# Two plain sums of a graph kernel: ten tiles each fetched row by row from the sync engine and ScalarE

## What is computed

```
agg = jax.ops.segment_sum(x[src], dst, num_segments=N)         # first layer
h = (1.0 + eps) * x + agg
...
h = x @ W                                                      # last layer
msg = h[src] * norm[:, None]
out = jax.ops.segment_sum(msg, dst, num_segments=N) + b
```

## Time and profile before

| | us |
|---|---|
| median of 3 runs | 9637.63 |
| profiled execution, its own time | 9643.64 |
| span of the profiled execution | 9641.6 |
| first sum with the plan, first gather to last | 18.6 to 1158.7 |
| last sum, first gather to last | 8450.3 to 9577 |
| GpSimd busy, whole span | 5742.4 |

### The profile page before, as it was taken

The page is one execution under the profiler, slowest core; times in us unless marked ns, Lnnn a source line. Parts: engine busy times, 40 slices in busy tenths (PEclk is TensorE's granted clock), DMA queues, the critical chain, the costliest instruction groups (busy, mean ns, idle before and its releaser), DMA issues. The chain is left out here.

```text
span 9641.6 us, 93453 instructions
## 1 busy us (share of the span) xinstructions
PE 5106.8 (53%) x23452; PEld 3485.5 (36%) x23571; DVE 5124.3 (53%) x19615; ACT 1985.2 (21%) x5001; POOL 5742.4 (60%) x5738
## 2 busy tenths in 40 slices
PE   2332332444414444497777777777767777623223
PEld 2222322433413333343233333333356667513213
DVE  3233443444524444676777777777766666724225
ACT  0000021222212222310222222222234444500001
POOL 6676526666456666122666666666556666466765
PEclk7555665555555555698888889989979998855556
DMA  2111122222122222287666667766656666221111
GB/s 64 46 47 46 38 45 59 72 70 68 48 63 70 69 68 67 66 334 259 199 203 207 199 205 208 208 203 204 183 163 175 176 176 176 73 54 45 47 46 46
DMA packets 434195, 1155.57 MB, mean 120 GB/s; under 512 B 106036, under 2 KB 147476, under 8 KB 420744
## 3 DMA queue, kind: packets, MB, share of 16 engines
q0 software_dynamic: 295984, 849.83, 32.1%
q1 hardware_dynamic: 122892, 275.01, 8.5%
q10 hardware_dynamic: 14796, 24.75, 0.8%
HBM read 1016.65 MB, written 132.52 MB: 119 GB/s over the span
## 5 line engine op out<-in xcount | busy, mean ns | idle before, releaser
L953 POOL DMA_INDIRECT gat_ring<-gat_table,psrc_idx x1664 | 1645.6, 989 | 1120.5 <-issue 476.0
L589 DVE TENSOR_TENSOR acc<-acc,bank 128x129 f32 (+1 forms) x1664 | 480.1, 289 | 1475.1 <-remote 1252.9
L1938 POOL DMA_INDIRECT pair<-right_table,idx_r_idx x782 | 799.5, 1022 | 582.3 <-issue 183.6
L1148 DVE TENSOR_TENSOR acc<-acc,bank 128x130 f32 x1664 | 482.5, 290 | 1214.0 <-remote 847.1
L2098 POOL DMA_INDIRECT msg<-left_table,pidx_idx x832 | 799.7, 961 | 502.5 <-issue 203.0
L1938 POOL DMA_INDIRECT acc<-left_table,idx_l_idx x782 | 802.6, 1026 | 428.8 <-issue 219.1
L521 POOL DMA_INDIRECT gcn_sum_ring<-gcn_table,src_idx x782 | 790.2, 1011 | 369.5 <-issue 229.8
L521 POOL DMA_INDIRECT gin_sum_ring<-in_x,src_idx x782 | 769.0, 983 | 373.5 <-issue 226.5
L1017 PE MATMUL bank<-gat_ring,gat_hot 128*128 128x130 f32 x3328 | 765.7, 406 | 385.4 <-DVE gat_hot L1137 254.1
L2000 ACT ACTIVATE positive<-acc 128x512 f32<-128x512 f32 x782 | 492.4, 630 | 2022.2 <-DVE acc L2028 1358.7
L1977 PE MATMUL bank<-pair,ident 128*128 128x512 f32 x1564 | 874.9, 643 | 1.9 <-issue 1.5
(11 more groups left out here) (554 smaller groups left out, 9355.0 us busy)
## 6 DMA issues: line engine op xcount, KB each, us to landing
gat_place<-local_rows SPq DMA_DIRECT2D x128, 416.0 KB
left_table<-rel_out SPq DMA_DIRECT2D x49, 1032.0 KB, 4.9
right_table<-rel_out SPq DMA_DIRECT2D x49, 1032.0 KB, 3.9
feat<-attr_rows SPq DMA_DIRECT2D x194, 256.0 KB
gat_ring<-gat_table,psrc_idx POOLq DMA_INDIRECT x1664
types<-type_rows SPq DMA_DIRECT2D x98, 256.0 KB
msg<-left_table,pidx_idx POOLq DMA_INDIRECT x832
gin_sum_ring<-in_x,src_idx POOLq DMA_INDIRECT x782
```

Source lines behind the costliest of these rows:

```text
L953: e.indirect_dma_start(ring[:, at:at + TROW], None, table[:, :], bass.IndirectOffsetOnAxis(ap=ed["psrc"][:, i:i + 1], axis=0)).then_inc(*g ...
L1938: e.indirect_dma_start(to[j % NG][:, n * LROW:(n + 1) * LROW], None, tab[:, :], bass.IndirectOffsetOnAxis(ap=idx[:, i:i + 1], axis=0)).the ...
```

## The change

In both sums the tiles 118, 190, ..., 766 are fetched by the sync engine and the tiles 82, 154, ..., 730 by ScalarE: ten tiles each, every 72nd. GpSimd leaves them out. A new class `Singles` first loads the ten tiles' source rows as a list into SBUF (one DMA, one tile per partition). For each of its tiles it waits for the slot as GpSimd does, then 16 times loads eight row numbers into registers of its engine and issues eight DMAs of one row of 512 bytes each, whose place in the table is the register's value. Each adds 16 to one of two semaphores in turn. PE waits for the 128 landings of a tile before the batch that begins with or holds it. `gathered` counts how many gathers of GpSimd a batch's semaphore gets now. In the first sum the sync engine does this after the plan's store and ScalarE at once; in the last sum the sync engine does it ahead of the stores of the output, and ScalarE between `first_scalar` and `Ending.scalar`. The lists lie in 1 KB per partition: their own in the first sum, a part of an index table that is no longer needed in the last. One scratch tile of the plan now shares its place with another.

```diff
--- before.py
+++ after.py
@@ -38,6 +38,7 @@
 CHUNKS = PAIRS // CT
 RING = 128
 PLAN_AT = 40
+SP_TILES, ACT_TILES = (118, TILES, 72), (82, TILES, 72)
 GR = 13
 HQ = 4
 PAIR = 2
@@ -197,8 +198,8 @@
         self.k, self.c, self.ed, self.recs, self.local_rows = k, c, ed, recs, local_rows
         self.rec = sb("rec_i", G * 3 * P, I32)
         self.tile_i, self.tile_f = sb("tile_i", IT, I32), sb("tile_f", IT)
-        self.limit_i, self.limit, self.below = (sb(n, NB * G, d) for n, d in (
-            ("limit_i", I32), ("limit", F32), ("below", F32)))
+        self.limit_i, self.limit = (sb(n, NB * G, d) for n, d in (("limit_i", I32), ("limit", F32)))
+        self.below = self.limit_i[:, :].bitcast(F32)
         self.cnt, self.begins, self.block_col = sb("cnt", NB), sb("begins", 1), sb("block_col", 2 * G)
         self.passed, self.blk, self.tau, self.local, self.psrc, self.pidx, self.ends = (
             acc[:, j * SLOTS:(j + 1) * SLOTS] for j in range(7))
@@ -493,6 +494,43 @@
 
 
 
+class Singles:
+
+
+    def __init__(self, k, name, tiles, recs, table, ring, idx):
+        self.k, self.tiles, self.table, self.ring = k, tiles, table, ring
+        self.lists = recs[tiles.start:tiles.stop:tiles.step, 0:P]
+        self.idx = idx
+        self.landed = k.slots(f"{name}_dma", 2)
+        (self.listed,) = k.begin("loaded")
+
+    def fetch(self, e, engine, product):
+        e.dma_start(self.idx[0:len(self.tiles), :], self.lists).then_inc(*self.listed.up(16))
+        e.wait_ge(*self.listed.at(2, 16))
+        for n, i in enumerate(self.tiles):
+            free = slot_free(i)
+            if free:
+                e.wait_ge(*product.at(free))
+            at = i % RING * TROW
+            for q in range(0, P, BATCH):
+                row = self.k.regs(engine, self.idx[n:n + 1, :], q, BATCH, N - 1)
+                for j in range(BATCH):
+                    e.dma_start(self.ring[q + j:q + j + 1, at:at + F], self.table[bass.ds(row[j], 1), :]
+                                ).then_inc(*self.landed[n % 2].up(16))
+
+    def wait_tile(self, e, i):
+        if i in self.tiles:
+            n = self.tiles.index(i)
+            e.wait_ge(*self.landed[n % 2].at((n // 2 + 1) * P, 16))
+
+
+def slot_free(i):
+
+    b = i // HQ
+    free = min((b + 1) * HQ, TILES) - 1 - RING + NB
+    return max(0, -(-free // HQ))
+
+
 def aggregate_rows(k, c, ed, name, table, acc, width, plan=None, end=None):
     with ExitStack() as own:
         NQ, Q, NH, NP2, NBATCH = 22, HQ, 3, 3, PAIRS // HQ
@@ -503,6 +541,11 @@
         premade = lambda b: ENDS <= b < ENDS + late
         hot_of = lambda b: hot[NH + b - ENDS if premade(b) else b % NH]
         got = k.slots("pool_dma", NQ)
+        lists = k.sb(f"{name}_lists", 2 * P, I32, ctx=own)[:, :] if plan else ed["idx_l"][:, 0:2 * P]
+        singles = {ENG.SP: Singles(k, "sp", range(*SP_TILES), ed["recs"], table, ring, lists[:, 0:P]),
+                   ENG.Activation: Singles(k, "act", range(*ACT_TILES), ed["recs"], table, ring, lists[:, P:2 * P])}
+        one_by_one = {i for s in singles.values() for i in s.tiles}
+        gathered = lambda b: sum(i not in one_by_one for a in range(b % NQ, b + 1, NQ) for i in range(a * Q, a * Q + size(a)))
         filled, hot_made, product, added, chained, end_made = k.begin(
             "filled", "hot_made", "product", "added", "dve", "meaned")
         size = lambda b: min(Q, TILES - b * Q)
@@ -514,25 +557,30 @@
             def _(e):
                 for i in range(TILES):
                     b = i // Q
-                    free = b * Q + size(b) - 1 - RING + NB
-                    if i % Q == 0 and free > 0:
-                        e.wait_ge(*product.at(-(-free // Q)))
+                    if i % Q == 0 and slot_free(i):
+                        e.wait_ge(*product.at(slot_free(i)))
                     at = i % RING * TROW
-                    e.indirect_dma_start(
-                        ring[:, at:at + F], None, table[:, :],
-                        bass.IndirectOffsetOnAxis(ap=ed["src"][:, i:i + 1], axis=0)).then_inc(*got[b % NQ].up(16))
+                    if i not in one_by_one:
+                        e.indirect_dma_start(
+                            ring[:, at:at + F], None, table[:, :],
+                            bass.IndirectOffsetOnAxis(ap=ed["src"][:, i:i + 1], axis=0)).then_inc(*got[b % NQ].up(16))
                     if plan and i == PLAN_AT - 1:
                         plan.gpsimd(e)
 
-            if plan or end:
-                @block.sync
-                def _(e):
-                    (plan or end).sync(e)
-
-            if end:
-                @block.scalar
-                def _(e):
+            @block.sync
+            def _(e):
+                if plan:
+                    plan.sync(e)
+                singles[ENG.SP].fetch(e, ENG.SP, product)
+                if end:
+                    end.sync(e)
+
+            @block.scalar
+            def _(e):
+                if end:
                     end.first_scalar(e, filled)
+                singles[ENG.Activation].fetch(e, ENG.Activation, product)
+                if end:
                     end.scalar(e, added)
 
             @block.tensor
@@ -542,7 +590,10 @@
                 e.wait_ge(*filled.at(2 if width > F else 1))
                 for b in range(NBATCH):
                     if b * Q < TILES:
-                        e.wait_ge(*got[b % NQ].at(b // NQ * Q + size(b), 16))
+                        e.wait_ge(*got[b % NQ].at(gathered(b), 16))
+                        for i in range(b * Q, b * Q + size(b)):
+                            for s in singles.values():
+                                s.wait_tile(e, i)
                     if b * Q % BATCH == 0:
                         at = k.regs(ENG.PE, ed["ring_row"], b * Q, BATCH, (RING - 1) * TROW)
                     e.wait_ge(*(end_made.at(b - ENDS + 1) if premade(b) else hot_made.at(b + 1 - (late if b > ENDS else 0))))
@@ -1302,12 +1353,12 @@
         turned, out_v, out_s, loaded, dve = k.begin("turned", "out_v", "out_s", "loaded", "dve")
         att_split, packed, widened, gated, exped, typed = k.begin(
             "att_split", "packed", "widened", "gated", "exped", "typed")
-        part_out = k.slots("part_out", 3)
+        part_out = k.slots("act_dma", 3)
         attr_got, cast, residual, weights, firsts, laters, linear = k.begin(
             "attr_got", "cast", "residual", "weights", "left_loaded", "right_loaded", "linear")
         folded, fold, product, biased, lin_product, lin_biased = k.begin(
             "folded", "fold", "product", "biased", "lin_product", "lin_biased")
-        stored = k.slots("row_out", 2)
+        stored = k.slots("sp_dma", 2)
         with k.nc.Block() as block:
             @block.sync
             def _(e):
@@ -2556,7 +2607,7 @@
     with ExitStack() as ctx:
         k = Kernel(nc, ctx)
         c = make_constants(k)
-        ed = {"degree": k.sb("degree", NB)}
+        ed = {"degree": k.sb("degree", NB), "recs": w["recs"]}
         x, acc = k.sb("x_rows", NP), k.sb("acc", NB * ROW)
         with ExitStack() as early:
             with ExitStack() as own:
```

## The result

The changed kernel takes 10237.1 us (median of 4 runs, 10220.4 to 10257.7), the kernel before 9634.4 beside it: ratio 1.0633, interval [1.0611, 1.0654]. The forecast was 9584, the range ended at 9740.

The account below looks back on a forecast made before the run. GpSimd's issuing of gathers was taken to bound both sums, not the bytes. Profiled 9643.6 us minus 54 for 40 gathers, with the row fetches hidden, gave 9589.6, or 9584 against the median; range 9555 to 9740.

Parts of the forecast that it names:

- (a): Both sums: 20 fewer GpSimd gathers each, at 1.35 us, save 27 us per sum, 54 us in all.
- (b): Sync and ScalarE, both sums: 1280 one-row DMAs each per sum, 0.5 us per row (0.40 to 0.89), 64 us per tile.
- (c): Both sums: slots free early enough to hide 64 us per tile; tightest lead 86 us, so nothing waits up to 0.67 us per row.
- (d): Side effects: ScalarE's late activations stay hidden, at most 16 us otherwise; PE's extra waits at most 1 us per sum.
- Rows too slow: Rival, both sums: at 0.89 us per row on ScalarE, 0.81 on Sync, PE waits; +150, 9788 us; chance 0.14.
- The new DMAs hold products back: Rival, both sums: Sync's and ScalarE's rows delay products too; slot waits half as long again, +51, 9689 us; chance 0.09.

Follow-up runs that it names:

- undelayed: Sessions where the kernel before takes 8314 to 8327 us; there the unchanged pair gave 8275.1 us for the changed kernel against 8323.6, ratio 0.9938.
- delayed: Sessions where the kernel before takes 9525 to 9634 us; there the changed kernel took 10237.1 us against 9634.4, ratio 1.0633.
- the fixed rows: Changed kernel with row DMAs taking fixed table rows, without register loads and address instructions (wrong rows fetched), against the kernel before: first 8266.5 us, 0.9945.

## Why the prediction was wrong

- **(a) The gathers removed** are worth what was said. Forecast 27 us per sum, measured undelayed 26.7 and 24.8. In the recorded run nothing of them is left, as GpSimd is no longer what the sums wait for.
- **(b) The cost of a row is the step that failed**: 0.5 us with bounds 0.40 and 0.89, measured 1.01 in the recorded run. Without the delay it is 0.52 (the load of eight 0.10 per row, not 0.07), so the forecast by the sum of instructions held there. The sentence that failed is "so the gathers do not slow the issue". It rested on the duration of line 962 in the earlier trace rows, 0.320 us, which is 0.320 in the undelayed trace as well. Those 128 DMAs come singly over 2600 us, and a duration does not show what an engine loses between its instructions: the rows' DMAs keep a median of 0.225 us while a row comes to take twice as long. The upper bound was also made of durations, and so fell short.
- **(c) The cover** was right as arithmetic. It named 0.80 us per row as the point from which the queues fall behind for good. By the same reckoning ScalarE's ten tiles of 130 us from 154 end at 1454 (measured 1445), Sync ends at 1502.5, and PE needs another 33.
- **(d)** The small things stayed small.
- **The rivals.** "Rows too slow" (0.14) is what happened. It was priced at 0.89 us and +150; by its own sum 1.01 us makes 1293 us per queue, so Sync ends at 204 + 1293 = 1497 and 8607 + 1293 = 9900 against the wants at 1208 and 9597, +592 in all, and +603 was measured. Its size was missed because its upper price was too low, and its reason ("both queues would be busy together") is not the one: undelayed both are busy and a tile takes 66 us. "The new DMAs hold products back" is not shown: in the first sum GpSimd's "remote" waits are 96.5 us for 107.0 before and DVE's are 502.2 for 602.5, and in undelayed sessions the rows disturb nothing. Its thought was the right one turned round: while GpSimd gathers, the new rows are held back as PE's products are.
- **What I should have asked.** The prediction wrote that the trace does not say what holds the products back, and then let it concern PE alone. An unexplained hold-up that coincides with GpSimd's gathers had to be priced for every new instruction put beside them: a batch of PE's 16 instructions was up to 20 us late, over 1 us each. At any such price a row of three instructions and an eighth of a load is no 0.5 us; what it came to is 0.16 us more per instruction, as many pass while GpSimd pauses.

What stays open: what makes a session delayed, and by what path the other engines are held back while GpSimd gathers. Every run here has its instructions or at least its clock recorded, and none shows the time without any recording, so that this takes part in the hold is not ruled out. The records number the chips, and number 5 was undelayed (8314) in one session and delayed (9525) in another ten minutes later; that speaks against a fixed property of a chip. Two of the nine sessions of the experiments were delayed, and the recorded comparison. Whether one instruction per row would have saved the change in such a session is not known: the fixed rows ran in six sessions, all of them undelayed.

## What to carry to other kernels

Take the price of an instruction on an idle engine from the pace, start to start, of instructions beside the same neighbours, not from its duration; an engine that is idle in the profile is not one that would run at full pace. If products are late in a trace for no visible reason, expect the same lateness of everything that is added beside the same engine's work. And measure a gain of 0.6% in several sessions: here one kernel pair gave 0.994 and 1.063, and neither is noise.

## Not expected

- The same program takes 8314 to 8327 us in seven sessions and 9525 to 9634 in the others, 14 to 16% more, with gathers of the same length (944 and 947 ns) and the same instruction count (93453).
- A queue's instructions beside gathers without a pause: 7.6 per gather within a tile undelayed, falling to about one per gather delayed, and 5.0 per us while GpSimd stands still. The held ones of both queues start together, in steps of 0.72 us or twice that.
- A load of eight registers takes ScalarE 0.83 and Sync 0.79 us, one of a single register 0.48. ScalarE's row DMA right behind a load of either kind takes 462 to 468 ns, the next ones 228 to 235.
